# A decoder layer's experts stage anew: routing in groups of six and two batches, results finished and stored in slot order

## The reference, cut to what matters

```python
probs = softmax(tokens @ gate_w)
mask1 = one_hot(argmax(probs), E)
pos = cumsum(mask1, axis=0) - 1
sec_mask = mask1[:, :, None] * one_hot(pos, CAP)        # tokens past CAP are dropped
expert_input = einsum('tec,td->ecd', sec_mask, tokens)
h = relu(einsum('ecd,edf->ecf', expert_input, w1))      # D 128, F 512
expert_output = einsum('ecf,efd->ecd', h, w2)
out = einsum('tec,ecd->td', probs[:, :, None] * sec_mask, expert_output)
x = layernorm(x + out)
```

## Time and profile before

| | |
|---|---|
| runs of the kernel | 376.27 us median (376.02 to 376.48) |
| the profiled execution, its own time | 379.05 us |
| its span | 377.3 us |
| PE, DVE, ACT, POOL busy | 80%, 76%, 65%, 52% of the span |
| mean granted clock of TensorE | 0.912 |
| stages (us from the span's start) | start 0 to 51, scans to 226, attention to 300, routing to 327, experts to 356, end to 377 |

### The profile page before, as it was taken

How to read it: one execution, slowest core, us unless ns; L and a number is a source line. 1 busy time by engine, 2 the same in 40 slices (tenths; PEclk the granted TensorE clock), 3 DMA queues, 4 the chain that set the end, 5 groups by cost and what they waited for, 6 DMA issues and landing times.

```text
span 377.3 us, 5352 instructions
## 1 busy us (share of the span) xinstructions
PE 301.1 (80%) x1677; PEld 183.7 (49%) x1677; DVE 287.2 (76%) x459; ACT 246.0 (65%) x445; POOL 196.9 (52%) x131
## 2 busy tenths in 40 slices
PE   4999917999999998999999999889999643099600
PEld 3444505555565645454554548446555532089600
DVE  2767798999999999999999995698887563012235
ACT  2359995999999998999999974758567410022100
POOL 7400547999999988988889840200000005400073
PEclk9999975999999999999999999999999875559955
DMA  6987022232233331323221000000000000200212
GB/s 158 311 250 224 13 63 96 66 112 97 73 111 105 117 105 66 114 112 108 76 97 56 3 0 2 1 0 2 2 2 1 0 2 28 83 16 17 54 43 70
DMA packets 16769, 26.91 MB, mean 71 GB/s; under 512 B 1965, under 2 KB 10309, under 8 KB 16741
## 3 DMA queue, kind: packets, MB, share of 16 engines
q1 hardware_dynamic: 16036, 25.46, 21.5%
q0 software_dynamic: 704, 1.10, 1.0%
HBM read 24.00 MB, written 2.56 MB: 70 GB/s over the span
## 4 chain that ended last, share of the span: by engine, by line
PE 39%; DVE 33%; issue 10%; POOL 9%; DMA 4%; ACT 3%; SPq 1%; POOLq 0%; DVEq 0%; ACTq 0%
DVE arena L1133 21%; PE bank L683 16%; POOL arena L445 6%; PE bank L721 4%; DVE acc L1143 3%; PE bank L1010 3%; PE bank L900 3%; PE bank L919 2%; PE bank L1018 2%; PE bank L819 2%; PE bank L743 2%; PE bank L709 2%; POOL arena L481 2%; ACT arena L651 2%; DMA cw<-in_L_attn_convb_w 1%
## 5 line engine op out<-in xcount | busy, mean ns | idle before, releaser
L445 POOL TENSOR_TENSOR arena<-arena,k_maskT 128x1024 f32<-128x1024 f32 x64 | 150.5, 2375 | 40.3 <-DVE arena L1120 22.6
L1133 DVE TENSOR_TENSOR_SCAN arena<-bank,arena 128x512 f32<-128x512 f32 x128 | 146.1, 1202 | 0.0
L683 PE MATMUL bank<-ident,arena 128*128 128x128 f32 (+1 forms) x726 | 110.8, 289 | 38.0 <-DVE arena L1133 14.3
L683 PEld LDWEIGHTS bank<-ident,arena 128*128 128x128 f32 (+1 forms) x726 | 82.1, 145 | 106.9 <-DVE arena L1133 60.8
L819 PE MATMUL bank<-conv_in_T,ident 128*128 128x512 f32 x192 | 93.7, 598 | 0.0
L545 ACT ACTIVATE bank<-delta,a_neg 128x508 f32<-128x508 f32 x128 | 88.3, 692 | 6.5 <-DVE arena L1133 5.7
L589 ACT ACTIVATE conv_in_T<-bank,c_col 128x256 f32<-128x256 f32 x192 | 80.3, 472 | 12.5 <-PE bank L683 11.8
L457 POOL TENSOR_SCALAR rstd<-moments 128x4 f32<-128x4 f32 x6 | 1.4, 242 | 83.5 <-DVE moments L1185 83.4
L819 PEld LDWEIGHTS bank<-conv_in_T,ident 128*128 128x128 f32 x192 | 31.8, 192 | 15.8 <-issue 15.0
L489 ACT ACTIVATE arena<-bank 128x512 f32<-128x512 f32 (+2 forms) x26 | 12.0, 489 | 33.0 <-PE bank L683 27.6
L1040 DVE COPY arena<-bank 128x160 f32<-128x160 f32 (+2 forms) x20 | 8.1, 433 | 31.1 <-PE bank L1018 17.2
(11 more groups left out here) (155 smaller groups left out, 298.6 us busy)
## 6 DMA issues: line engine op xcount, KB each, us to landing
k_maskT<-b_rows SPq DMA_DIRECT2D x32, 512.0 KB, 3.7
w_sb<-in_L_ffn_w SPq DMA_DIRECT2D x1, 2048.0 KB, 11.1
dispatched_tokens<-zeros SPq DMA_DIRECT2D x1, 640.0 KB, 16.6
expert_outputs<-arena SPq DMA_DIRECT2D x4, 160.0 KB, 2.1
x_tok<-in_x SPq DMA_DIRECT2D x1, 512.0 KB, 3.8
ctx_tok<-in_ctx SPq DMA_DIRECT2D x1, 512.0 KB, 4.2
out<-arena SPq DMA_DIRECT2D x2, 256.0 KB, 2.3
arena<-dispatched_tokens SPq DMA_DIRECT2D x1, 384.0 KB, 3.8
```

The costliest lines, as they stand in the source:

```text
L445: gp.tensor_tensor(dBx[g % 2][h], du[:, dr, h, :], b_bc[:, g % RING, :], ALU.mult).then_inc(dBx_ok, 1)
L683: return pe.transpose(dst, src, ident[0:src.shape[0], 0:src.shape[0]])
L1133: ve.tensor_tensor_scan(o, a, v, 0.0, ALU.mult, ALU.add).then_inc(scanned, 1)
```

## The change

The core of the diff; where a hunk is left out, the text under it says what it does.

```diff
-    ROUTE0 = 2 * B + 1
+    ROUTES = ((0, B - 2), (B - 2, B))
+    EXTRA = CAP - P
+    PER_B = P // EXTRA
+    ROW = D + 2
-        xe_in = [sem(f"xe_in{k}") for k in range(2)]
+        LOADS = ((E, ST), (0, 1), (1, 2), (2, 4), (4, E))
+        FINISH = ((0, 1), (2, 3, E), (4, 5), (6,), (7, E + 1))
@@ SP
             sp.wait_ge(dispatched, 16 * B)
+            for k, (first, last) in enumerate(LOADS):
+                sp.dma_start(xe[:, first:last, :], d_xe[:, first:last, :]).then_inc(xe_in[k], 16)
+            sp.wait_ge(alone_ok, B)
+            sp.dma_start(out.rearrange("b s d -> s b d"), y_alone).then_inc(alone_out, 16)
@@ POOL
+                for b in range(first, last):
+                    gp.indirect_dma_start(d_slots, bass.IndirectOffsetOnAxis(slot_u[:, b:b + 1], 0), x2[:, b, :], None,
+                                          bounds_check=SLOTS - 1, oob_is_err=False).then_inc(dispatched, 16)
+            rstd_of(2, 0, 0, B)
+            gp.wait_ge(alone_out, 16)
+            for tiles_now in FINISH:
+                gp.wait_ge(tile_var_ok, done)
+                link(gp.tensor_scalar(tile_rstd[:, first:last], tile_moments[:, first:last, 1], EPS, None, ALU.add))
+                gp.tensor_tensor(tile_rstd[:, first:last], tile_rstd[:, first:last], neg_half[:, first:last],
+                                 ALU.pow).then_inc(tile_rstd_ok, 1)
+                for at, j in enumerate(tiles_now):
+                    gp.wait_ge(tile_ok, first + at + 1)
+                    gp.indirect_dma_start(out_rows, bass.IndirectOffsetOnAxis(token_u[:, j:j + 1], 0), y_tile[:, first + at, :],
+                                          None, bounds_check=T - 1, oob_is_err=False).then_inc(stored, 16)
@@ ACT, attention: the exponential (L642) moves behind the copy (L651)
-                if i < 2 * B:
-                    wait_read(sc, f"s{i}")
-                    sc.activation(prob[i % 3], prob[i % 3], ACT.Exp, scale=SCALE).then_inc(exp_ok, 1)
...
+                if i < 2 * B:
+                    wait_read(sc, f"s{i}")
+                    sc.activation(prob[i % 3], prob[i % 3], ACT.Exp, scale=SCALE).then_inc(exp_ok, 1)
@@ PE
+            def keep_busy(k, times):
+                for _ in range(times):
+                    turn(bank[:, k, 0:P], ident[:, :])
             pe.wait_ge(ident_ok, 1)
+            keep_busy(0, 14)
             pe.wait_ge(x_in, 16)
...
+            wait_read(pe, held_at_scan[HT_BANK])
+            keep_busy(HT_BANK, 50)
             for g in range(STEPS):
@@ DVE, attention
+                ve.tensor_reduce(rmax[:, c, :], src, AX.X, ALU.max).then_inc(dve, 1)
+                if i % 2 == 1 and i >= 7:
+                    add_residual(i // 2 - 3)
+                ve.wait_ge(dve, max_done)
@@ DVE, experts
+            for b in range(B):
+                moments_of(x2, b)
+            normalize(x2, y_alone, 2, 0, 0, B, alone_ok)
+            def finish_tile(j):
+                was_read(f"eo{j}", ve.scalar_tensor_tensor(res3[:, at, :], src[:, 0:D], xe[:, j, D:D + 1], xe[:, j, 0:D],
+                                                           ALU.mult, ALU.add))
+                link(ve.bn_stats(tile_stats[:, at, :], res3[:, at, :]))
+                ve.bn_aggr(tile_moments[:, at, :], tile_stats[:, at, :]).then_inc(tile_var_ok, 1)
+            def store_tiles(k):
+                ve.wait_ge(tile_rstd_ok, k + 1)
+                for at in range(first, first + len(FINISH[k])):
+                    ve.tensor_scalar(y_tile[:, at, :], res3[:, at, :], tile_moments[:, at, 0:1], tile_rstd[:, at:at + 1],
+                                     ALU.subtract, ALU.mult).then_inc(tile_ok, 1)
```

More of the change, by code:

```diff
@@ L130, in decoder_layer_kernel @@
         route_b = sb("route_b", [P, 8, B])
[L131 removed]
+        zeros = sb("zeros", [P, ROW])
         tri = sb("tri", [P, P], BF16)
@@ L943, in gate_logits @@
             def gate_logits(g):
-                pe.wait_ge(x2_ok, HB * (g + 1))
-                turn_group(f"x2T{g}", [x2[:, b, :] for b in range(HB * g, HB * g + HB)])
+                first, last_b = ROUTES[g]
+                pe.wait_ge(x2_ok, last_b)
+                to_fill(pe, f"x2T{g}")
+                flat = bank[:, where[f"x2T{g}"][0]:where[f"x2T{g}"][0] + 2, :].rearrange("p a t -> p (a t)")
+                for b in range(first, last_b):
+                    last = turn(flat[:, S * (b - first):S * (b - first) + S], x2[:, b, 0:D])
+                filled(f"x2T{g}", last)
                 pe.wait_ge(moe_w_in, 48)
@@ L948, in gate_logits @@
                 wait_read(pe, f"x2T{g}")
-                for b in range(HB):
-                    t0 = TH * g + S * b
-                    last = pe.matmul(dst[:, E * b:E * b + E], x2T[:, t0:t0 + S], gate[:, :], start=True, stop=True)
+                for b in range(first, last_b):
+                    last = pe.matmul(dst[:, E * (b - first):E * (b - first) + E], x2T[:, S * b:S * b + S], gate[:, :],
+                                     start=True, stop=True)
                 filled(f"logits{g}", last)
             def count_tokens(g):
-                pe.wait_ge(consts_ok, 6)
+                first, last_b = ROUTES[g]
+                many = last_b - first
+                pe.wait_ge(consts_ok, 5)
                 pe.wait_ge(route_mask, g + 1)
@@ L1021, in _ @@
                 if e >= 2:
-                    wait_read(pe, f"eoT{e - 2}")
-                    dst = to_fill(pe, f"eo{e - 2}")
-                    for s in range(2):
-                        last = turn(dst[0:HC, D * s:D * s + D], eoT[e % 2][:, HC * s:HC * s + HC])
-                    filled(f"eo{e - 2}", last)
+                    done, k = e - 2, E + (e - 2) // PER_B
+                    at = EXTRA * (done % PER_B)
+                    wait_read(pe, f"eoT{done}")
+                    dst = to_fill(pe, f"eo{done}")
+                    extra = to_fill(pe, f"eo{k}") if at == 0 else bank[:, where[f"eo{k}"][0], :]
+                    last = pe.matmul(extra[at:at + EXTRA, 0:D], eoT[done % 2][:, P:CAP], ident[:, :], start=True, stop=True)
+                    if at + EXTRA == P:
+                        filled(f"eo{k}", last)
+                    filled(f"eo{done}", turn(dst[:, 0:D], eoT[done % 2][:, 0:P]))
         @block.vector
@@ L1183, in moments_of, with normalize @@
             def moments_of(res, b):
[L1184 removed]
+                link(ve.bn_stats(stats[:, b, :], res[:, b, 0:D]))
                 ve.bn_aggr(moments[:, b, :], stats[:, b, :]).then_inc(var_ok, 1)
[L1187 removed]
+            def normalize(res, dst, norm, g, first, last, done):
                 ve.wait_ge(rstd_ok, 2 * norm + g + 1)
[L1189 to L1190 removed]
+                for b in range(first, last):
+                    ve.tensor_scalar(dst[:, b, 0:D], res[:, b, 0:D], moments[:, b, 0:1], rstd[:, b:b + 1],
                                      ALU.subtract, ALU.mult).then_inc(done, 1)
```

279 lines of the change are left out of this document (137 added, 142 removed).

## The result

The changed kernel takes **370.32 us** (median; 369.2 to 371.32), the kernel before 376.21 beside it (376.02 to 376.48): ratio 0.984, interval 0.981 to 0.987. It is faster by 5.9 us, where 15.25 were forecast, and 370.3 lies outside the range of 355.5 to 368.5. Its profiled execution took 371.32 us with a span of 369.5; a second one (its runs 371.16 us, ratio 0.989, 0.985 to 0.993) has a span of 369.4.

A forecast was written before the change was run, and what follows sets the result against it. Bound by stage: PE to 51 us, DVE in the scans, PE in attention, short steps in line from 297. Terms -4.2 -0.5 -0.4 -1.55 -2.8 +3.1 -8.9 = -15.25 gave a median of 361.0 us, range 355.5 to 368.5.

The forecast's parts named there:

- the first term: Start, before the scans: fourteen identity turns before x arrives raise PE's clock at 5 to 8 us, saving 4.2 us.
- Rival (a): Start and before the scans: identity turns don't raise PE's clock, time 369.2 us; chance 0.13.
- Before the scans: Fifty identity turns on PE keep the clock up and give back most of DVE's 1.26 us stall: -0.5 us.
- Attention: Attention loop: residual no longer delays DVE's maximum, ACT copies before its exponential; 6.6 us per batch against 6.92, -0.4 us.
- Routing: Last attention turns to routed rows landed, in groups of 6 and 2: 28.3 us against 29.85, -1.55 us.
- To the first expert: Routed rows landed to first expert matmul: fewer loads, turns and copies ahead, 3.65 us against 6.45, -2.8 us.
- Experts: Expert stage on PE: two added turns and an fp32 matmul make each expert dearer, +3.1 us in all.
- Tail: Last turn to end: last HBM write and gathers gone, POOL's roots and scatters in line, 12.9 us against 21.8, -8.9 us.
- Rival (b): Indirect DMAs: the bounds check puts them 1.6 us apart, +6.1 us over 18, time 367.1 us; chance 0.10.
- the forecast's own range: Whole kernel: 357.5 to 365 us for the main forecast, from half the sum of its parts' bounds; chance 0.65.

## Why the prediction was wrong

Two steps failed above all: the price of an expert's small instructions on PE, and the first term, which counted the late clock of one execution a second time. The figures in brackets are the forecast and the change by the two second profiles.

**The start (-4.2, -1.3).** What failed is the reading of the earlier trace rows as the kernel's own state. That profiled execution got its clock at 17 us, another at 10.8, and the changed kernel without the turns at 8. The times had said it: its own time was 2.8 us above the median. The forecast took these 2.8 off at the end, and took the same lateness off once more as the first term. That is a double count of about 2.9 us. Rival (a) was tested as a mechanism by the eighty turns and fell: turns alone raise the clock. The Trainium skill (TensorE: Matmul & The Clock Gate, Part 4: PE-mode transpose), which says that the full clock doesn't engage for them, doesn't hold here, by the windows from 311 to 319. Yet its time, 369.2, was nearer to the result than mine, because the term was missing for another reason.

**Before the scans (-0.5, +0.25).** The fifty turns took 8.55 us and DVE waited 1.62 for PE's turns behind them, within the bounds given. In the twelve profiles with them the stretch is 14.5 us in the mean, without them 14.4, so the saving of 0.5 from a clock that is up again isn't there.

**Attention (-0.4, -1.65).** The step that was mis-sized is the later iterations: I laid out 3.17 and 3.42 in turn, 6.6 a batch, since ACT's line of copy and exponential was put on the path throughout. From the fifth group on PE is full at 6.35, and ACT is beside it. The first iterations came as forecast (3.15).

**Routing (-1.55, -0.2).** Worked out were 17.0 us from the last group to the slots, 9.1 to the last scatter and 2.2 to its landing. Measured: 17.3 (the six turns 1.49, the gate logits 2.70, at the slow clock as laid out), 10.1 and 2.3. The step that failed is the handover to POOL: the 9.1 us leave 0.3 for it beside seven steps of 1.26, and it measured 0.98; then the second scatter starts 1.45 behind the first and the others stand 1.28 apart.

**To the first expert (-2.8, -2.67).** Right: 3.60 against 3.65.

**Experts (+3.1, +10.65).** This is the step that failed. Its price was durations times counts: 0.22 for two turns, 0.37 for a turn and an fp32 matmul of 128 columns, with the second half of each pair taken from rows of 128x128. I gave no bound for it, although the attention's rows of 32 columns, shown above, had 0.17 and 0.20 us of idle weight path around them, some 3 us over eight experts (an estimate: 8 x 0.37). Measured: 3.25 instead of 2.75 for a steady expert, of which 0.57 are changes of shape. Over eight experts that makes about 4 us; 2.6 more are PE's wait for DVE at the last turn, which the prediction had named as what would make it wrong, but had not priced in the experts' own stage. The rest, about 1 us, belongs to the first experts at half clock. The forecast had the slow stretch the same length in both kernels; from the first expert matmul to the rise it is 4.4 us before (333.5 to 337.9) and 7.7 after (325.0 to 332.7), with turns, a copy and a wait of 0.39 us for it in line.

**Tail (-8.9, -10.2).** From the last turn on it is 12.1 us against 12.9 (11.6 from its end, as the forecast counted): right, and for the reason given, POOL and DVE in one line. What was overlooked is that this line reaches back into the experts. A root costs 0.58, 0.72 or 0.89 us for one, two or three columns, less than the 1.04 for four in the earlier trace rows, and scatters without the check gave 1.6 us. Rival (b) had the check costing 6.1 us, 0.34 between scatters; measured are 0.5 behind each wait and nearly nothing between scatters.

**The range.** By the rule given, half of the sum of the parts' bounds, the forecast's own range comes out as 356.9 to 367.8, not 357.5 to 365. The expert's price had no bound in it at all, and the largest miss lay there.

## What to carry to other kernels

Before a profile is costed, compare its own time with the median: an execution 2.8 us above it shows a state that an edit can't take away a second time. An instruction with 32 rows or columns on PE costs, beside itself, the weight loads that no longer hide, so surplus rows are better gathered into a whole tile by the engines that copy anyway (2.40 us an expert against 3.25). And an engine that makes a small value for another (the roots here) must not have long work queued ahead of it: moving ten roots from POOL to ACT, each tile finished by itself, gave 4.7 us in the trace and 6.0 between the medians, where the whole change gave 5.9.

## What was not expected of the hardware

- Eighty turns of the identity bring the granted clock from 0.50 to 1.00. The kernel before got the full clock 10.8 us after its start in one execution and 17.0 in another.
- A weight load of 32 rows, one of 32 columns and the one after 32 columns aren't hidden: 0.17 to 0.20 us idle each, 0.14 net per change in the mean. Loads of 80 columns are.
- In the tail an indirect DMA with a bounds check starts 0.80 us after what it waits for, without one 0.29.
- Ln and Exp of one column on ACT take 0.29 and 0.20 us, POOL's addition and power 0.24 and 0.58.
